# Graph attention on one core: run penalties built with fewer vector operations, one message tile moved from ScalarE to VectorE, and the third group of q rows moved ahead of the message sums on TensorE

## The chip, the cores and the metric

The kernel runs on one core of one Trainium2 chip. The metric is the device time in microseconds of one execution of the whole program. The engines are named as the profile names them: PE is TensorE (PEld its weight loads), DVE is VectorE, ACT is ScalarE, POOL is GpSimd, SP is SyncE.

## What is computed

A graph has 3125 nodes with 512 features and 50,000 edges (src, dst). Two layers follow each other; each normalises its input, applies relu and adds its result to the input. The change lies in the first layer, the attention, cut here to what matters:

```
q = (h @ Wq + bq).reshape(N, DH, NH)          # N=3125, 8 heads of 64
k = (h @ Wk + bk).reshape(N, DH, NH);  v = k
scores = einsum('edh,edh->eh', q[rows], k[cols])
m = segment_max(scores, rows)
ex = exp(scores - m[rows])
attn = ex / segment_sum(ex, rows)[rows]
out = segment_sum(attn[:, None, :] * v[cols], rows)
return out @ Wo + bo
```

The second layer sums the node rows over the other end of the edges, divides by the degree and applies two weight matrices.

## The kernel before, in words

**Stages.** The program first makes q (as three bf16 parts that add up to the f32 value) and k for all nodes, while DVE sorts the edges by node (roughly the first 385 us). Then comes the attention stage, up to about 1240 us, then the output weights, then the second layer. The change touches only the attention stage.

**Chunks.** The sorted edges are cut into windows of 125 destination nodes, and each window into chunks of CAP = 2176 edges: 128 partitions times CT = 17 tiles, with an edge's run of equal nodes lying along a partition and crossing into the next. There are 25 rounds of the function `attend` here, one for each chunk, on each engine. Round g works on two chunks at once: the scores of chunk g, and the messages (k row times weight) and their sums of chunk g-1. The order is written out by hand in each engine's block, and semaphores tie the engines together.

**One round on DVE** (`attend`, L1322 to L1381): `decode` of the next chunk's edge words (L1226 to L1235); `merge` of the former window's sums (L1304 to L1312); `messages` for the first MT = 3 tiles (L1294, two operations, one for each half of the heads); then nine groups of q rows. A group is two tiles (the last one tile). For each, L1339 multiplies the q rows in PSUM with the gathered k rows, and L1348 sums the products of the group before over the 64 features. Once the product of a group is seen to be complete, `wide_free` (L1347) lets PE overwrite its buffer. Then two scans along the partition (L1355, L1356) find the maximum of each run, with penalties of -1e30 where a run ends; `flags` (L1245 to L1263) makes the penalties for the next chunk in ten operations; two short scans (L1363, L1364) carry the maxima from partition to partition; and L1372 to L1376 add the carried maxima with their penalties, take the largest of three values and subtract it from the scores. That releases ACT (`res_ready`).

**One round on PE** (L819 to L855): two transposes for the penalties (L823), then for each of the nine groups the q rows, picked with a one-hot matrix of the edges (L834: 3 parts x 2 tiles = 6 matmuls), followed by SEG[n] tiles of message sums (L806: a tile is two matmuls, recorded as four since f32 takes two passes). The q rows alternate between two PSUM buffers, wide0 and wide1, so a group waits until DVE has finished with the group two before it (L831). After the fifth index (n == 5) come two small products for the fading factors (L816, L817). After the last group PE has two transposes (L846, L847), two more tiles, two transposes back (L851, L852) and the last four tiles.

**ACT** makes the messages of the tiles from MT to 16 with eight operations a tile (L621), and scales the window's sums (L630, L640). **POOL** gathers the k rows of the next chunk, one tile an instruction (L497), in the four parts of PARTS, and builds the one-hot tiles of the next sum (L521). A part of the row buffer is gathered only when the messages that read it are made: part 0 is released by DVE (L1343), the others by ACT (L658, L662, L667).

```
Q_GROUPS = [(t, min(2, CT - t)) for t in range(0, CT, 2)]
MT = 3
SEG = [0, 2, 1, 1, 1, 1, 1, 1, 3]
PARTS = [(0, 3), (3, 4), (7, 5), (12, CT - 12)]
```

## Time and profile before

| | us |
|---|---|
| median of 3 runs | 1978.0 (1966.38 to 1984.02) |
| the profiled execution, its time | 1975.45 |
| the profiled execution, its span | 1973.6 |
| busy in the span: PE / DVE / ACT / POOL | 1652.9 / 1367.9 / 990.9 / 1143.6 |
| mean granted TensorE clock | 0.943 of full speed |

The span runs from the first to the last instruction of the profiled execution; its own time is 1.85 us longer, for what lies around it. Times of rows are microseconds from the start of the span, a duration given as a mean is in ns. In a row of the timeline, neighbouring instructions of one kind are merged: the start, the length from the first start to the last end, and the count. An end of a matmul is modelled, and instructions of one engine overlap by a little, so a step is best read from start to start.

### The profile page before, as it was taken

Reading aid. Unit: us, or ns where it says so; the run is one execution under the profiler, and the core shown is the slowest. Engines: PE = TensorE matmul, PEld = TensorE weight load, DVE = VectorE, ACT = ScalarE, POOL = GpSimd, SP = SyncE. Lnnn points to the kernel's source line nnn. Section 1 sums busy time; section 2 is a strip of 40 time slices with the busy share of each in tenths; the row PEclk is TensorE's granted clock in tenths of the full one; section 3 lists DMA queues with packets and bytes.
Section 4 is the critical chain, followed back from the end, with each engine's and each line's share of the span. In section 5 each row is a group of like instructions: output and inputs, shape, how many; then the busy total and the mean of one; then the engine's idle time right before and its main releaser. Section 6 shows DMA issues by size and latency. Waiting matters only on the chain.

```text
span 1973.6 us, 23860 instructions
## 1 busy us (share of the span) xinstructions
PE 1652.9 (84%) x5685; PEld 953.0 (48%) x5685; DVE 1367.9 (69%) x2637; ACT 990.9 (50%) x3754; POOL 1143.6 (58%) x1322
## 2 busy tenths in 40 slices
PE   3799942289888888898889887895999999999998
PEld 1343321166666666666666666342444444444443
DVE  8789878598988898889888985465444444444441
ACT  4453310559999999999999997241000000000000
POOL 2000000487878787878787880014777777777772
PEclk9899976599999999999999999897999999999999
DMA  8122201655565656565656562935777777776773
GB/s 183 52 66 78 65 26 52 195 153 160 165 183 165 184 166 187 162 183 160 182 166 183 157 177 67 230 97 157 213 221 215 215 212 217 211 207 208 213 212 97
DMA packets 130752, 318.05 MB, mean 161 GB/s; under 512 B 39460, under 2 KB 39710, under 8 KB 130596
## 3 DMA queue, kind: packets, MB, share of 16 engines
q0 software_dynamic: 70240, 229.93, 40.6%
q1 hardware_dynamic: 60356, 86.43, 15.6%
q8 instruction: 50, 0.82, 0.2%
q14 instruction: 106, 0.87, 0.1%
HBM read 280.43 MB, written 35.86 MB: 160 GB/s over the span
## 4 chain that ended last, share of the span: by engine, by line
PE 45%; DVE 23%; DMA 13%; issue 13%; ACT 2%; SPq 2%; DVEq 1%; POOL 1%; POOLq 0%; ACTq 0%
PE wide L754 15%; PE sums L806 10%; PE wide L834 8%; PE sums L903 8%; DMA node<-h2tab 5%; DMA out<-node 4%; DVE arena L1057 3%; DVE arena L1056 3%; DVE nodes L1348 2%; DMA h2tab<-node 2%; DVE nodes L1294 1%; DVE nodes L1339 1%; DVE node L1235 1%; PE wide L749 1%; ACT arena L575 1%
## 5 line engine op out<-in xcount | busy, mean ns | idle before, releaser
L621 ACT ACTIVATE nodes<-arena,nodes 128x64 f32<-128x64 f32 x2840 | 682.7, 332 | 1.3 <-PE sums L806 1.2
L497 POOL DMA_INDIRECT arena<-ktab,idx x425 | 425.6, 1001 | 174.1 <-issue 116.3
L497 POOL DMA_INDIRECT arena<-h2tab,idx x425 | 444.8, 1047 | 140.9 <-issue 133.0
L806 PE MATMUL sums<-nodes,oh 128*125 128x260 f32 x1768 | 459.0, 402 | 41.9 <-DVE nodes L1294 41.9
L754 PE MATMUL wide<-w_sb,node 128*125 128x512 f32 x1000 | 469.5, 614 | 12.7 <-ACT node L560 9.1
L806 PEld LDWEIGHTS sums<-nodes,oh 128*125 128x125 f32 x1768 | 336.8, 195 | 116.7 <-DVE nodes L1294 53.3
L903 PE MATMUL sums<-arena,oh 128*125 128x512 f32 x850 | 373.6, 597 | 7.6 <-DMA arena<-h2tab,idx 7.6
L701 ACT ACTIVATE node<-wide 128x500 f32<-128x500 f32 x51 | 28.9, 586 | 582.6 <-PE wide L889 582.4
L834 PE MATMUL wide<-q_win,node 125*128 125x512 bf16 x1275 | 311.1, 382 | 8.4 <-issue 8.4
L754 PEld LDWEIGHTS wide<-w_sb,node 128*125 128x125 f32 x1000 | 185.6, 194 | 227.2 <-issue 209.7
L1339 DVE TENSOR_TENSOR nodes<-wide,arena 128x1024 f32<-128x1024 f32 (+1 forms) x225 | 258.7, 1159 | 12.5 <-PE wide L834 11.8
L1348 DVE TENSOR_REDUCE nodes<-nodes 128x16 f32<-128x1024 f32 (+1 forms) x225 | 256.9, 1151 | 0.0
L903 PEld LDWEIGHTS sums<-arena,oh 128*125 128x125 f32 x850 | 157.8, 188 | 203.4 <-issue 191.9
L521 POOL TENSOR_SCALAR oh<-iota,loc 128x125 f32<-128x125 f32 x425 | 245.5, 593 | 0.8
L1449 DVE SCALAR_TENSOR_TENSOR acc<-acc,first_chunk,sums 125x512 f32<-125x512 f32 x25 | 18.7, 748 | 315.2 <-PE sums L903 315.2
L834 PEld LDWEIGHTS wide<-q_win,node 125*128 125x128 bf16 x1275 | 177.9, 141 | 98.6 <-issue 12.3
L503 POOL DMA_DIRECT2D sorted_tab<-arena x2 | 1.2, 610 | 325.5 <-DVE arena L1103 325.5
L1057 DVE TENSOR_TENSOR arena<-arena 128x256 f32<-128x256 f32 x272 | 114.0, 419 | 0.0
L1056 DVE TENSOR_TENSOR arena<-arena 128x256 f32<-128x256 f32 x272 | 113.9, 419 | 0.0
L1397 DVE TENSOR_REDUCE junk<-oh 128x125 f32<-128x2125 f32 x25 | 104.1, 4163 | 0.9
L533 POOL DMA_DIRECT2D h2tab<-node x25 | 13.4, 535 | 151.9 <-ACT node L685 140.9
L1242 DVE TENSOR_TENSOR oh<-iota,loc 128x2125 f32<-128x2125 f32 x25 | 59.3, 2373 | 4.0 <-DVE loc L1233 4.0
(199 smaller groups left out, 1157.6 us busy)
## 6 DMA issues: line engine op xcount, KB each, us to landing
node<-node_tab SPq DMA_DIRECT2D x27, 531.2 KB
q_win<-qtab SPq DMA_DIRECT2D x26, 375.0 KB
arena<-ktab,idx POOLq DMA_INDIRECT x425, 5.8
arena<-h2tab,idx POOLq DMA_INDIRECT x425, 4.5
node<-h2tab SPq DMA_DIRECT2D x26, 250.0 KB
attn_tab<-win_out SPq DMA_DIRECT2D x25, 250.0 KB
h2tab<-node POOLq DMA_DIRECT2D x25, 250.0 KB, 2.9
out<-node SPq DMA_DIRECT2D x25, 250.0 KB
```

What stands on the lines that cost most here:

```text
L497: gp.indirect_dma_start(rows[:, b, t, :], None, tab, bass.IndirectOffsetOnAxis(ap=idx[:, b, t:t + 1], axis=0)).then_inc(s["rows_in"][b][PA ...
L521: last = gp.tensor_scalar(oh[:, b, t, :], iota[:, 0:WIN], loc[:, b, t + 1:t + 2], None, ALU.is_equal)
L621: last = act.activation(msgs[:, t, h // HH, h % HH * DH:(h % HH + 1) * DH], rows[:, 1 - b, t, h * DH:(h + 1) * DH], ACT.Copy, scale=den_in ...
L754: last = pe.matmul(out, ncol[:, b, c, :], w_sb[:, w, c, :], start=start and c == 0, stop=stop and c == KC - 1)
L806: last = pe.matmul(halves[:, u, :], oh[:, 1 - b, t, :], rhs[side][:, t, u, :], start=t == 0, stop=t == CT - 1)
L834: last = pe.matmul(wide[n % 2][:, (t - t0) * D:(t - t0 + 1) * D], ohT[:, b, :].rearrange("p (e t) -> p t e", t=CT)[:, t, :], q_win[:, b, p ...
L903: last = pe.matmul(aggp, oh[:, b, t, :], rows[:, b, t, :], start=t == 0, stop=t == CT - 1)
L1056: self.made(dve.tensor_tensor(new[:, :, 0, :], old[:, :, 0, :], old[:, :, 1, :], ALU.min))
L1057: self.made(dve.tensor_tensor(new[:, :, 1, :], old[:, :, 0, :], old[:, :, 1, :], ALU.max))
L1339: made.append(st.mark(dve.tensor_tensor(prod[:, n % 3, 0:k * D], wide[n % 2][:, 0:k * D], rows[:, b, t0:t0 + k, :].rearrange("p t d -> p ( ...
L1348: summed.append(st.mark(dve.tensor_reduce(sc[:, :, t0:t0 + k].rearrange("p h t -> p t h"), prod[:, (n - 1) % 3, 0:k * D].rearrange("p (t h ...
L1397: dve.tensor_reduce(oh_sum[:, b, :], oh[:, b, :, :].rearrange("p t n -> p n t"), AX.X, ALU.add).then_inc(ag["kept"], 1)
```

## The change

1. `flags` makes the penalties in five operations instead of ten. One vector `links` of 8 x 17 + 1 values per chunk, read from its first element by the forward scan and from its second by the backward scan, takes the place of two arrays of 8 x 17. The two comparisons with the end tiles become one operation, as do the two side penalties, and PE's transposes read a side penalty directly with a broadcast instead of a copy of it (`whole` is gone).
2. The two maxima `top` = max(carried0, carried1) and max(top, over) become one `tensor_reduce` over a view `three` that has the three arrays side by side in memory, 136 elements (544 bytes) apart.
3. MT goes from 3 to 4: DVE makes four message tiles, ACT thirteen. PARTS follows.
4. SEG goes from [0, 2, 1, 1, ...] to [0, 0, 2, 2, 1, ...]: PE makes the third group of q rows before any message sum, and two tiles of sums follow both the third and the fourth group. The total before the transposes stays 11 tiles.

```diff
@@ -96,15 +96,15 @@
         junk = sb("junk", [128, 2, HALF])
         scratch = junk[:, :, :].rearrange("p a c -> p (a c)")
         SEGS = CT * H
-        pen = scratch[:, 0:4 * SEGS].rearrange("p (b k h t) -> p b k h t", b=2, k=2, h=H)
-        seg_max, over, top = (scratch[:, k * SEGS:(k + 1) * SEGS].rearrange("p (h t) -> p h t", h=H) for k in (4, 5, 6))
+        links = scratch[:, 0:2 * (SEGS + 1)].rearrange("p (b s) -> p b s", b=2)
+        seg_max, top, over = (scratch[:, k * SEGS:(k + 1) * SEGS].rearrange("p (h t) -> p h t", h=H) for k in (4, 5, 6))
+        three = scratch[:, 6 * SEGS:9 * SEGS].rearrange("p (k s) -> p s k", k=3)
         carried = scratch[:, 7 * SEGS:9 * SEGS].rearrange("p (k h t) -> p k h t", k=2, h=H)
         AT = 9 * SEGS
         sides_pen = scratch[:, AT:AT + 4 * CT].rearrange("p (b k t) -> p b k t", b=2, k=2)
         same = scratch[:, AT + 4 * CT:AT + 4 * CT + CT + 1]
         same_end = scratch[:, AT + 5 * CT + 1:AT + 7 * CT + 1].rearrange("p (k t) -> p k t", k=2)
-        whole = scratch[:, AT + 7 * CT + 1:AT + 7 * CT + 1 + 4 * H].rearrange("p (b k h) -> p b k h", b=2, k=2)
-        ROWS_AT = AT + 7 * CT + 1 + 4 * H
+        ROWS_AT = AT + 7 * CT + 1
         whole_T = scratch[0:H, ROWS_AT:ROWS_AT + 256].rearrange("p (k n) -> p k n", k=2)
         from_left = scratch[0:H, ROWS_AT + 256:ROWS_AT + 256 + 2 * 129].rearrange("p (b n) -> p b n", b=2)
         from_right = scratch[0:H, ROWS_AT + 514:ROWS_AT + 514 + 129]
@@ -216,7 +216,7 @@
         QK_TURNS = [NW - 3, NW - 2]
         KEY_TURNS = [(238, 1), (251, 0), (271, 0), (286, 0)]
 
-        PARTS = [(0, 3), (3, 4), (7, 5), (12, CT - 12)]
+        PARTS = [(0, 4), (4, 3), (7, 5), (12, CT - 12)]
         PART = [max(n for n, (t0, k) in enumerate(PARTS) if t0 <= t) for t in range(CT)]
 
         def chunk_sems(p):
@@ -240,9 +240,10 @@
         fade_ready, faded_ready, others_ready, alpha_turned, alpha_ready = (sem(n) for n in ("fade_ready", "faded_ready", "others_ready", "alpha_turned", "alpha_ready"))
 
         Q_GROUPS = [(t, min(2, CT - t)) for t in range(0, CT, 2)]
-        MT = 3
+        MT = 4
+        WHOLE = (CT - 1, 0)
         TT = 12
-        SEG = [0, 2, 1, 1, 1, 1, 1, 1, 3]
+        SEG = [0, 0, 2, 2, 1, 1, 1, 1, 3]
         MID_SEG = 2
         EARLY = sum(SEG)
         assert len(SEG) == len(Q_GROUPS) and MT <= EARLY
@@ -820,7 +821,7 @@
                 pe.wait_ge(whole_ready, g + 1)
                 pe.wait_ge(alpha_ready, g + 1)
                 for k in range(2):
-                    last = pe.transpose(whole_turn[:, k, :], whole[:, b, k, :], ident[:, :])
+                    last = pe.transpose(whole_turn[:, k, :], sides_pen[:, b, k, WHOLE[k]:WHOLE[k] + 1].to_broadcast([128, H]), ident[:, :])
                 last.then_inc(whole_turned, 1)
 
                 todo = iter(range(CT))
@@ -1244,27 +1245,22 @@
 
             def flags(g, b):
 
-                st = Steps(flag_step, g, 10)
+                st = Steps(flag_step, g, 5)
                 here = loc[:, b, 1:CT + 1]
                 st.mark(dve.tensor_tensor(same, loc[:, b, 1:CT + 2], loc[:, b, 0:CT + 1], ALU.is_equal))
-                for k, t in enumerate((0, CT - 1)):
-                    st.mark(dve.tensor_scalar(same_end[:, k, :], here, here[:, t:t + 1], 1.0, ALU.is_equal, ALU.subtract))
+                st.mark(dve.tensor_tensor(same_end, here.unsqueeze(1).to_broadcast([128, 2, CT]), here[:, ::CT - 1].unsqueeze(2).to_broadcast([128, 2, CT]), ALU.is_equal))
                 st.seen(1)
-                st.then(dve.tensor_scalar(same, same, 1.0, BIG, ALU.subtract, ALU.mult))
-                for k, link in enumerate((same[:, 0:1], same[:, CT:CT + 1])):
-                    st.mark(dve.scalar_tensor_tensor(sides_pen[:, b, k, :], same_end[:, k, :], BIG, link.to_broadcast([128, CT]), ALU.mult, ALU.add))
+                st.then(dve.tensor_scalar(same, same, BIG, 2 * BIG, ALU.mult, ALU.subtract))
+                st.mark(dve.scalar_tensor_tensor(sides_pen[:, b, :, :], same_end, BIG, same[:, ::CT].unsqueeze(2).to_broadcast([128, 2, CT]), ALU.mult, ALU.add))
                 inside = same[:, 1:CT].unsqueeze(1).to_broadcast([128, H, CT - 1])
-                st.mark(dve.tensor_copy(pen[:, b, 0, :, 1:CT], inside))
-                st.mark(dve.tensor_copy(pen[:, b, 1, :, 0:CT - 1], inside))
-                st.seen(6)
-                st.mark(dve.tensor_copy(whole[:, b, 0, :], sides_pen[:, b, 0, CT - 1:CT].to_broadcast([128, H])))
-                st.then(dve.tensor_copy(whole[:, b, 1, :], sides_pen[:, b, 1, 0:1].to_broadcast([128, H])))
+                st.mark(dve.tensor_scalar(links[:, b, 0:SEGS].rearrange("p (h t) -> p h t", h=H)[:, :, 1:CT], inside, BIG, None, ALU.add))
+                st.seen(5)
                 st.end()
                 dve.sem_inc(whole_ready, 1)
 
             dve.wait_ge(consts, 3)
             firsts = [(res[:, :, :], 0.0), (acc[:, :], 0.0), (rden[:, :], 0.0), (fade[:, :], 0.0), (others[:, :, :], 0.0),
-                      (scratch[:, 0:4 * SEGS], -BIG), (from_left[:, :, :], -BIG), (from_right, -BIG)]
+                      (links[:, :, :], -BIG), (from_left[:, :, :], -BIG), (from_right, -BIG)]
             for b in range(2):
                 dve.wait_ge(store1[b], STORE1 * ((NW + 1 - b) // 2))
             for v, value in firsts:
@@ -1320,7 +1316,7 @@
                     merge(g, 1)
 
             def attend(g, b, i):
-                st = Steps(at["step"], g, 2 * len(Q_GROUPS) + 10)
+                st = Steps(at["step"], g, 2 * len(Q_GROUPS) + 9)
                 decode(at, g + 1, 1 - b, i + b, 5, 4)
                 merge_former(g, b, i)
                 dve.wait_ge(msgs_free, g + 1)
@@ -1352,8 +1348,8 @@
                 def line(v):
                     return v.rearrange("p h t -> p (h t)")
 
-                st.then(dve.tensor_tensor_scan(line(seg_max), line(pen[:, b, 0, :, :]), line(sc), -BIG, ALU.add, ALU.max))
-                st.then(dve.tensor_tensor_scan(line(over)[:, ::-1], line(pen[:, b, 1, :, :])[:, ::-1], line(seg_max)[:, ::-1], -BIG, ALU.add, ALU.max))
+                st.then(dve.tensor_tensor_scan(line(seg_max), links[:, b, 0:SEGS], line(sc), -BIG, ALU.add, ALU.max))
+                st.then(dve.tensor_tensor_scan(line(over)[:, ::-1], links[:, b, 1:SEGS + 1][:, ::-1], line(seg_max)[:, ::-1], -BIG, ALU.add, ALU.max))
                 dve.sem_inc(seg_ready, 1)
 
                 flags(g + 1, 1 - b)
@@ -1371,8 +1367,7 @@
                 dve.wait_ge(carry_turned, g + 1)
                 st.then(dve.tensor_tensor(carried, carry.unsqueeze(3).to_broadcast([128, 2, H, CT]),
                                           sides_pen[:, b, :, :].unsqueeze(2).to_broadcast([128, 2, H, CT]), ALU.add))
-                st.then(dve.tensor_tensor(top, carried[:, 0, :, :], carried[:, 1, :, :], ALU.max))
-                st.then(dve.tensor_tensor(top, top, over, ALU.max))
+                st.then(dve.tensor_reduce(line(top), three, AX.X, ALU.max))
                 st.then(dve.tensor_tensor(res[:, :, :], sc[:, :, :], top, ALU.subtract))
                 dve.sem_inc(res_ready, 1)
                 dve.wait_ge(faded_ready, g + 1)
```

PE, from the transposes at the head of a round (L823 before, L824 after) to the sixth group of q rows. L834 and L835 are the q rows, L806 and L807 the message sums; wide0 and wide1 are the two PSUM buffers. Before:

```order
L823 MATMUL wide2<-ident,junk 8x128 x2
L834 MATMUL wide0<-q_win,node 128x512 x6
L834 MATMUL wide1<-q_win,node 128x512 x6
L806 MATMUL sums<-nodes,oh 125x260 x4
L834 MATMUL wide0<-q_win,node 128x512 x6
L806 MATMUL sums<-nodes,oh 125x260 x2
L834 MATMUL wide1<-q_win,node 128x512 x6
L806 MATMUL sums<-nodes,oh 125x260 x2
L834 MATMUL wide0<-q_win,node 128x512 x6
L806 MATMUL sums<-nodes,oh 125x260 x2
L834 MATMUL wide1<-q_win,node 128x512 x6
```

After:

```order
L824 MATMUL wide2<-ident,junk 8x128 x2
L835 MATMUL wide0<-q_win,node 128x512 x6
L835 MATMUL wide1<-q_win,node 128x512 x6
L835 MATMUL wide0<-q_win,node 128x512 x6
L807 MATMUL sums<-nodes,oh 125x260 x4
L835 MATMUL wide1<-q_win,node 128x512 x6
L807 MATMUL sums<-nodes,oh 125x260 x4
L835 MATMUL wide0<-q_win,node 128x512 x6
L807 MATMUL sums<-nodes,oh 125x260 x2
L835 MATMUL wide1<-q_win,node 128x512 x6
```

The third group (the second wide0) now stands ahead of the first two tiles of sums (x4 is two tiles). The sixth group has five tiles of sums ahead of it in both; the two small products and one more tile follow it, and then the seventh group, unchanged.

DVE, from the second scan of the scores to the copy ahead of the carrying scans, before:

```order
L1356 SCALAR_TENSOR_TENSOR junk<-junk 128x136
L1249 TENSOR_TENSOR junk<-loc 128x18
L1251 TENSOR_SCALAR junk<-loc 128x17 x2
L1253 TENSOR_SCALAR junk<-junk 128x18
L1255 SCALAR_TENSOR_TENSOR junk<-junk 128x17 x2
L1257 COPY junk<-junk 128x8x16
L1258 COPY junk<-junk 128x8x16
L1260 COPY junk<-junk 128x8
L1261 COPY junk<-junk 128x8
L1360 COPY junk<-junk 8x1
```

After:

```order
L1352 SCALAR_TENSOR_TENSOR junk<-junk 128x136
L1250 TENSOR_TENSOR junk<-loc 128x18
L1251 TENSOR_TENSOR junk<-loc 128x34
L1253 TENSOR_SCALAR junk<-junk 128x18
L1254 SCALAR_TENSOR_TENSOR junk<-junk 128x34
L1256 TENSOR_SCALAR junk<-junk 128x8x16
L1356 COPY junk<-junk 8x1
```

Ten instructions between the scan and the copy (x2 counts as two) have become five.

DVE, from `others` to `fade` at the end of a round, before and after:

```order
L1369 SCALAR_TENSOR_TENSOR others<-oh,first_chunk 1x125
L1372 TENSOR_TENSOR junk<-wide,junk 128x272
L1374 TENSOR_TENSOR junk<-junk 128x136
L1375 TENSOR_TENSOR junk<-junk 128x136
L1376 TENSOR_TENSOR nodes<-nodes,junk 128x136
L1379 TENSOR_TENSOR fade<-junk 1x8
```

```order
L1365 SCALAR_TENSOR_TENSOR others<-oh,first_chunk 1x125
L1368 TENSOR_TENSOR junk<-wide,junk 128x272
L1370 TENSOR_REDUCE junk<-junk 128x136
L1371 TENSOR_TENSOR nodes<-nodes,junk 128x136
L1374 TENSOR_TENSOR fade<-junk 1x8
```

L1374 and L1375 before are L1370 after, a reduce that reads 3 x 136 values and writes 136.

## Rows read from the trace of the kernel before

**Rows 1.** Busy us of each engine in one round of the attention stage

```profile
core 0: us, PE busy (x) PEld busy (x) DVE busy (x) ACT busy (x) POOL busy (x), PEclk, DMA share, GB/s
...
711.72:744.16 32.44, 28.05 (x131) 20.42 (x130) 28.89 (x52) 31.58 (x133) 26.79 (x35) 1.00 0.62 175
```

**Rows 2.** Waits, 412 to 1172 us: engine, line, releaser, total, times, longest

```profile
PE wide L846 <- DVEq L1357: 52.2, 24, 2.3
ACT nodes L646 <- DVEq L1377: 39.4, 23, 13.8
...
POOL arena L497 <- DVEq L1343: 31.6, 22, 3.6
...
DVE nodes L1339 <- PE wide L834: 8.7, 23, 0.5
```

**Rows 3.** Timeline of DVE, round from 711.72 us: start, length, row

```profile
715.20 1.83 DVE L1294 TENSOR_TENSOR nodes<-arena,nodes 128x768 f32<-128x768 f32 x2 [0.32 <-DVE rden L1312]
716.94 2.35 DVE L1339 TENSOR_TENSOR nodes<-wide,arena 128x1024 f32<-128x1024 f32 x2
...
730.07 1.22 DVE L1339 TENSOR_TENSOR nodes<-wide,arena 128x1024 f32<-128x1024 f32 x1 [0.18 <-PE wide L834]
...
732.34 1.21 DVE L1339 TENSOR_TENSOR nodes<-wide,arena 128x1024 f32<-128x1024 f32 x1
```

**Rows 4.** Timeline of PE, same round

```profile
712.96 2.76 PE L834 MATMUL wide<-q_win,node 125*128 125x512 bf16 x12
717.08 2.02 PE L806 MATMUL sums<-nodes,oh 128*125 128x260 f32 x8 [1.36 <-DVE nodes L1294]
718.93 1.46 PE L834 MATMUL wide<-q_win,node 125*128 125x512 bf16 x6
...
728.43 1.46 PE L834 MATMUL wide<-q_win,node 125*128 125x512 bf16 x6
```

**Rows 5.** Event that frees a q buffer, L1347 (not a busy time)

```profile
L1347 DVEq EVENT_SEMAPHORE  x15: 21/21/21, 718.3 to 762.6; - x15
```

**Rows 6.** Timeline of DVE at the end of the attention stage

```profile
1207.79 6.90 DVE L1294 TENSOR_TENSOR nodes<-arena,nodes 128x1024 f32<-128x1024 f32 x6 [0.32 <-DVE rden L1312]
```

**Rows 7.** Timeline of DVE, flags and the end of the same round

```profile
738.41 0.18 DVE L1249 TENSOR_TENSOR junk<-loc 128x18 f32<-128x18 f32 x1 [0.24 <-DVE junk L1356]
...
738.78 0.17 DVE L1253 TENSOR_SCALAR junk<-junk 128x18 f32<-128x18 f32 x1
739.10 0.26 DVE L1255 SCALAR_TENSOR_TENSOR junk<-junk 128x17 f32<-128x17 f32 x2
739.28 0.22 DVE L1257 COPY junk<-junk 128x128 f32<-128x128 f32 x1
...
740.10 0.14 DVE L1360 COPY junk<-junk 8x1 f32<-8x1 f32 x1 [0.25 <-DVE junk L1261]
...
742.28 0.30 DVE L1374 TENSOR_TENSOR junk<-junk 128x136 f32<-128x136 f32 x1
...
743.23 0.30 DVE L1376 TENSOR_TENSOR nodes<-nodes,junk 128x136 f32<-128x136 f32 x1
```

**Rows 8.** Two reduces of DVE by line, shortest, median and longest in ns

```profile
L1397 DVE TENSOR_REDUCE junk<-oh x25: 4125/4166/4189, 1353.3 to 1917.9; 128x125 f32<-128x2125 f32 x25
...
L1348 DVE TENSOR_REDUCE nodes<-nodes x225: 673/1210/1217, 390.8 to 1197.2; 128x16 f32<-128x1024 f32 x100, 128x8 f32<-128x512 f32 x13
```

**Rows 9.** Timeline of PE, waits followed by slow or by full-speed matmuls

```profile
738.60 1.92 PE L806 MATMUL sums<-nodes,oh 128*125 128x260 f32 x8
...
935.56 0.28 PE L846 MATMUL wide<-ident,junk 128*8 128x128 f32 x1 [2.17 <-DVEq L1357]
...
935.78 3.47 PE L806 MATMUL sums<-nodes,oh 128*125 128x260 f32 x8
...
388.68 3.83 PE L806 MATMUL sums<-nodes,oh 128*125 128x260 f32 x8 [8.44 <-DVE nodes L1294]
...
1210.20 17.96 PE L806 MATMUL sums<-nodes,oh 128*125 128x260 f32 x68 [3.52 <-DVE nodes L1294]
```

## The prediction

> **What bounds the kernel now.** I first read the page's busy shares by slice and the starts of the rounds of `attend`: only the attention stage is touched, and its round, the stretch from 711.72 to 744.16 us, is 32.44 us. The busy times of this round come next [rows 1]: ACT 31.58, DVE 28.89, PE 28.05, POOL 26.79 plus its gather issues. ACT looks like the bound, but the list of waits says otherwise [rows 2]: ACT waits in every round for DVE's subtraction (L1377; 39.4 us over 23 rounds), POOL waits in every round for DVE's release of part 0 (L1343; 31.6 us), and PE waits for DVE's scans (L1357; 52.2 us over 24 rounds). DVE waits for another engine in one place only that counts: 23 times, 8.7 us in all, for q rows from PE (L1339 after L834). Its other idle time is behind its own instructions. So the round is DVE's chain of instructions, with PE's q rows as a second chain that it meets on the way.
>
> Where the two meet is seen in the two timelines of one round. DVE starts the two message products at 715.20, the first q product at 716.94 and the seventh at 730.07 [rows 3]: 13.13 us. Product and reduce take 2.27 us start to start when nothing is late (730.07 to 732.34 [rows 3]). From the first product to the third DVE has two products and one reduce, three steps of half of that, 3.4 us, and from there to the seventh four pairs, 9.1 us: 12.5 us in all. So DVE is about 0.6 us late by the seventh product, and it is PE that makes it late: the seventh group of q rows starts at 728.43 and lasts 1.46 us [rows 4], to 729.89, 0.18 us before the product. PE in turn works without a break from 717.08, where it had waited 1.36 us for the messages, and the two tiles of sums that it then makes take 1.85 us, up to the third group of q rows at 718.93 [rows 4].
>
> **The change part by part.**
>
> *The fourth message tile on DVE.* Two operations of 128x768 elements take 1.74 us start to start (715.20 to 716.94 [rows 3]). At 128x1024 six of them take 6.90 us [rows 6], 1.15 us each, so two take 2.30. DVE's first q product moves back by 0.55 us, from 716.94 to 717.49. ACT loses eight operations, 1/14 of its messages; since it waits for DVE already [rows 2], that buys nothing by itself. POOL's wait for part 0 is there today; the release comes 0.55 us later in the round, and a longer round gives POOL that time back: nothing. The k rows of a part are gathered in the round before, so the fourth tile of part 0 is not waited for.
>
> *The third group of q rows first.* It goes into the buffer of the first group, so it cannot start before DVE's first product is complete. The event that says so is at 718.3 [rows 5], 1.36 us after the product's start at 716.94. After the change it comes at 717.49 + 1.36 = 718.85, and PE starts about 0.05 us later, as it did behind the messages (715.20 + 1.83 = 717.03, PE at 717.08 [rows 3, 4]). So the third group starts at 718.9: exactly when it starts today, 718.93. But today two tiles of sums are done by then; after the change PE has stood still in that time and both are still to do. Every group from the fifth on has as many tiles ahead of it as before, so each starts later by two tiles. A tile is 0.87 us (eight sums of two tiles: 1.85 us less the first one's 0.1 [rows 4]), so PE comes to the seventh group at 728.43 + 1.75 = 730.18, and DVE's seventh product at 730.18 + 1.46 + 0.18 = 731.82, against 730.07: +1.75 us. DVE alone would be there at 717.49 + 12.5 = 730.0, so PE decides. The 0.55 us of the messages lie inside the 1.75. What follows the seventh product keeps its distance from it. PE's wait before L846, 2.2 us in the mean (52.2/24 [rows 2]), is the cover for its own last sums and stays. Bounds: at least +1.2 (if one tile more than I think is hidden under the wait), at most +1.9.
>
> *Flags.* Today 1.69 us pass from L1249 (738.41) to L1360 (740.10) [rows 7]. After it: the comparison ends at 738.59 and is seen 0.14 us later, 738.73; the next step takes 0.32 (738.78 to 739.10 [rows 7]), 739.05; the side penalties need 0.12 to issue, the `links` operation lasts 0.22 as L1257 does, and 0.25 of waiting follow: 739.64. That is 0.46 us less. Bounds -0.3 and -0.6. It is on DVE's chain, so it counts in full; the transposes that the carrying scans need are done at 738.8, and PE's next wait (L851) has 0.9 us of cover.
>
> *The reduce in place of two maxima.* Today 0.95 us from L1374 to L1376 [rows 7]. The reduce reads 408 values. By L1348, which reads contiguous values at 1.04 ns each, (1210 - 676 for 512 more), it lasts 0.57 us and with 0.15 until the next step 0.72: a gain of 0.23. By L1397, which also reduces over a long stride (500 bytes), it is 4166/2125 = 1.96 ns each [rows 8], 0.80 us and with 0.15 us 0.95: nothing gained. The form is that of L1397 (here 544 bytes), so I take 0. The Trainium skill, SBUF — State Buffer, in "Door 1: The DMA port swizzle", says that accesses that leave a 16-byte line each time pay a penalty, which speaks for the slow price and against this edit; L1397's 1.96 ns agree with it.
>
> *Sum of this.* 1.75 - 0.46 + 0 = +1.3 us a round. The first round starts with slow matmuls and its own order of waits; I count it as nothing. 24 rounds x 1.3 = +31 us.
>
> *TensorE's clock.* PE's wait ahead of the third group grows from 1.36 us to 718.9 - 715.72 (the end of the first twelve, 712.96 + 2.76 [rows 4]) = 3.2 us. The rows show what waits do: behind the 2.17 us before L846 the eight sums sometimes take 3.47 us instead of 1.92 (935.78 and 738.60 [rows 9]), that is the lower level, 1.2 GHz, for most of them; I count 10 of the 25 such waits of the stage with over 2.5 us behind them. Behind the waits of 3.52 and 8.44 us it was slow both times (68 sums in 17.96 us, 8 in 3.83 us [rows 9]); behind 1.36 us never (2.02 us for 8 [rows 4]). A wait of 3.2 us lies between: from 10 of 25 to all of them, and I take 18. The price is 0.7 to 1.8 us (sums of 2.6 to 3.8 us against 2.0), 1.3 in the middle, and this time it falls on the third group and the sums behind it, PE's unbroken run up to the seventh group, so it reaches DVE in full. 18 x 1.3 = +23 us. The Trainium skill, TensorE: Matmul & The Clock Gate, in "HAM oscillation — how this bites in real kernels", warns of just this, bursts behind waits that each begin at the lower clock; the 3.47 us of the trace agree.
>
> Together 31 + 23 = +54 us. Against the profiled execution's own time, 1975.45, this gives 2029.5; the median of the runs is 2.5 us above that execution, so 2032.
>
> **Rivals.**
>
> *The clock holds.* As forecast, but the 3.2 us wait costs no more than its length. For it: over half of the 2.2 us waits had no effect. Against: 3.52 us did. 1978 + 31 = 2009 us.
>
> *Faster: PE is not what makes DVE late.* The mechanism is the meeting at the third and seventh groups. If PE could keep ahead with the third group made first, DVE would lose the 0.6 us of lateness that it has today, and the round would change by +0.55 (messages) - 0.6 (lateness) - 0.46 (flags) - 0.23 (reduce at the contiguous price) = -0.75 us, 24 times: 1978 - 18 = 1960 us. It decides if the seventh group is ready by 730.0, that is if PE's run from the third group on takes 9.5 us instead of 11.3. For it: DVE's only lateness is against PE today, and the third product stops being at risk. Against: PE's rows show no gap in that run that could close.
>
> *Nothing measurable.* The messages of the tiles behind MT, made earlier by ACT, could not help PE; but PE might start the third group earlier than the event suggests, and the reduce be cheap: +1.2 - 0.6 - 0.23 = +0.4 us a round without a clock effect, 1978 + 9 = 1987 us.
>
> *The change doesn't reach the order.* The listing of PE's instructions shows the third group moved, so this is left at nothing.
>
> **How the numbers follow.** Slower with the clock effect 0.48, slower with the clock held 0.26, nothing measurable 0.13, faster 0.13. The predicted time is that of the first, 2032. The range: below, it reaches past the clock held with the cheap reduce (2009 - 6) to the third case, 1985; above, all 25 waits slow at 1.5 us and the larger bounds, 31 + 37 + 5 = +73, 2051. It leaves out the faster case and some of the third. A measurement of this kernel can tell about 1% from no change, 20 us: faster than 1958 gets 0.1 (most of the faster case and a little for what I don't see), within 1% 0.2 (the rest of that case, the third case and a part of the second), slower than 1998 0.7.
>
> **What would show it.** In the new trace the round grows from 32.5 to 33.8 us where the clock is full and by more where it falls; PE's wait ahead of its third group is about 3.2 us and ends with DVE's event behind the first product; DVE waits for q rows at the fourth or fifth and at the seventh group, 1.8 us a round together where it was 0.6; flags takes 1.2 us; the reduce lasts 0.8 us (0.57 if the stride costs nothing); ACT's wait ahead of L646 grows to over 4 us. It would be wrong if PE's third group started within 1 us of the first product's start, or if DVE's waits for q rows were not longer than before.

## The result and the profile after

| | before | after |
|---|---|---|
| median of 4 runs, us | 1978.42 (1966.38 to 1984.02) | 2032.72 (2028.53 to 2046.07) |
| profiled execution, us | 1975.45 | 2028.53 |
| granted clock, mean of the span | 0.943 | 0.93 |

The ratio is 1.0283 (95% interval 1.0249 to 1.0316): the changed kernel is 54 us slower. Ratios, here and below, compare executions in the faster state of the chip; one execution of flags and reduce alone (e10, below), 2194.37 us at a granted clock of 0.778, is left out of its ratio by that. The loss lies in the attention stage; the last stretch is 3 us shorter. Stretches of the two kernels, columns as in [rows 1], after and then before, the middle one being that stage:

```profile
0.00:385.00 385.00, 234.48 (x598) 102.28 (x598) 315.78 (x818) 137.83 (x346) 31.06 (x36) 0.84 0.31 86
385.00:1291.50 906.50, 766.59 (x3291) 554.99 (x3291) 733.17 (x1161) 733.72 (x3060) 647.87 (x837) 0.93 0.53 155
1291.50:2026.60 735.10, 675.89 (x1796) 309.92 (x1796) 322.54 (x503) 71.30 (x151) 458.81 (x450) 0.98 0.69 196
```

```profile
385.00:1235.50 850.50, 738.27 (x3292) 539.71 (x3293) 730.12 (x1316) 780.68 (x3255) 654.33 (x837) 0.97 0.57 166
```

The stage has grown from 850.5 to 906.5 us, and TensorE's mean granted clock in it has gone from 0.97 to 0.93. The busy times of the page, after:

```profile
PE 1677.0 (83%) x5685; PEld 967.2 (48%) x5685; DVE 1371.5 (68%) x2482; ACT 942.8 (47%) x3554; POOL 1137.7 (56%) x1322
...
PEclk9899975699999999999999999898899999999999
```

DVE is as busy as before (1371.5 against 1367.9 us), ACT has 48 us less to do, PE 24 us more with the same instructions. Nobody has more work; the waits have grown. The list of waits over the same 23 or 24 rounds, columns as in [rows 2]:

```profile
ACT nodes L647 <- DVEq L1372: 131.0, 23, 13.3
...
POOL arena L498 <- DVEq L1339: 89.2, 22, 5.2
...
PE wide L835 <- DVEq L1343: 63.9, 23, 3.4
...
DVE nodes L1335 <- PE wide L835: 59.2, 77, 2.4
PE wide L847 <- DVEq L1353: 52.1, 24, 2.2
...
DVE junk L1368 <- PE wide L853: 8.0, 14, 0.9
```

Against [rows 2]: DVE's waits for q rows (L1339, now L1335) have gone from 8.7 to 59.2 us, and PE has a new wait of 63.9 us (L835 behind L1343), the one ahead of the third group; ACT's wait has grown from 39.4 to 131.0 us, which shows that its relief bought nothing. One round in which the clock held ahead of the third group, DVE first, then PE, columns as in [rows 3, 4, 7]:

```profile
1056.49 2.36 DVE L1290 TENSOR_TENSOR nodes<-arena,nodes 128x1024 f32<-128x1024 f32 x2 [0.31 <-DVE rden L1308]
1058.77 2.35 DVE L1335 TENSOR_TENSOR nodes<-wide,arena 128x1024 f32<-128x1024 f32 x2
...
1064.94 1.22 DVE L1335 TENSOR_TENSOR nodes<-wide,arena 128x1024 f32<-128x1024 f32 x1 [0.44 <-PE wide L835]
...
1067.99 1.22 DVE L1335 TENSOR_TENSOR nodes<-wide,arena 128x1024 f32<-128x1024 f32 x1 [0.70 <-PE wide L835]
...
1073.06 1.22 DVE L1335 TENSOR_TENSOR nodes<-wide,arena 128x1024 f32<-128x1024 f32 x1 [0.46 <-PE wide L835]
...
1081.46 0.18 DVE L1250 TENSOR_TENSOR junk<-loc 128x18 f32<-128x18 f32 x1 [0.24 <-DVE junk L1352]
...
1081.79 0.18 DVE L1253 TENSOR_SCALAR junk<-junk 128x18 f32<-128x18 f32 x1
...
1082.68 0.14 DVE L1356 COPY junk<-junk 8x1 f32<-8x1 f32 x1 [0.24 <-DVE junk L1256]
...
1084.84 0.44 DVE L1368 TENSOR_TENSOR junk<-wide,junk 128x272 f32<-128x272 f32 x1 [0.64 <-PE wide L853]
1085.42 0.62 DVE L1370 TENSOR_REDUCE junk<-junk 128x136 f32<-128x408 f32 x1
1086.19 0.30 DVE L1371 TENSOR_TENSOR nodes<-nodes,junk 128x136 f32<-128x136 f32 x1
```

```profile
1054.92 2.75 PE L835 MATMUL wide<-q_win,node 125*128 125x512 bf16 x12
1060.20 1.51 PE L835 MATMUL wide<-q_win,node 125*128 125x512 bf16 x6 [2.52 <-DVEq L1343]
1061.55 1.92 PE L807 MATMUL sums<-nodes,oh 128*125 128x260 f32 x8
...
1066.35 1.46 PE L835 MATMUL wide<-q_win,node 125*128 125x512 bf16 x6
...
1071.42 1.46 PE L835 MATMUL wide<-q_win,node 125*128 125x512 bf16 x6
...
1081.43 0.28 PE L847 MATMUL wide<-ident,junk 128*8 128x128 f32 x1 [2.21 <-DVEq L1353]
...
1081.65 2.84 PE L807 MATMUL sums<-nodes,oh 128*125 128x260 f32 x8
```

The third group starts at 1060.20, 1.43 us after DVE's first product (1058.77), as the event allows; the seventh product comes at 1073.06, 14.29 us after the first, where it was 13.13 [rows 3]. DVE waits three times on the way, 0.44, 0.70 and 0.46 us. Flags takes 1.22 us (1081.46 to 1082.68), where it took 1.69 [rows 7], and the reduce with its step 0.77 us where two maxima took 0.95. The round, from one start of `attend` to the next, is 34.20 us. In other rounds the clock falls behind PE's wait ahead of the third group:

```profile
600.88 2.55 PE L835 MATMUL wide<-q_win,node 125*128 125x512 bf16 x6 [3.03 <-DVEq L1343]
```

Its six matmuls take 2.55 us instead of 1.51, the sums behind them are slow too, and one of DVE's waits for q rows grows from 0.44 to 1.49 us:

```profile
607.31 1.22 DVE L1335 TENSOR_TENSOR nodes<-wide,arena 128x1024 f32<-128x1024 f32 x1 [1.49 <-PE wide L835]
```

From the first to the seventh product this round takes 15.97 us. That distance is 14.29 or 14.30 us in 11 of the 24 rounds after the first and 15.9 to 17.1 us in the other 13, 23.2 us more in sum.

The sum over 23 rounds closes. The mean round (first and last start 419.67 and 1226.69 us after, 417.81 and 1172.58 before) has gone from 32.82 to 35.09 us, +2.27. The parts are +0.54 (fourth tile: 1056.49 to 1058.77 is 2.28 us, against 1.74 in [rows 3]), -0.47, -0.18, (59.2 - 8.7)/23 = +2.20 for the waits for q rows and (8.0 - 3.5)/23 = +0.20 for the waits of L1368: +2.29.

### The profile page after: what moved, and what is told of

Same layout as the page of the kernel before. It is cut to its first block, busy times and chain, and to the rows that moved or that the text cites. A ratio compares the mean times of both kernels' runs of the same rounds, so it can differ in the third digit from the quotient of the medians.

```text
span 2026.6 us, 23454 instructions
## 1 busy us (share of the span) xinstructions
PE 1677.0 (83%) x5685; PEld 967.2 (48%) x5685; DVE 1371.5 (68%) x2482; ACT 942.8 (47%) x3554; POOL 1137.7 (56%) x1322
## 4 chain that ended last, share of the span: by engine, by line
PE 46%; DVE 21%; issue 14%; DMA 12%; POOL 3%; ACT 2%; SPq 2%; DVEq 1%; POOLq 0%; ACTq 0%
PE wide L755 14%; PE sums L807 13%; PE wide L835 9%; PE sums L904 7%; DMA node<-h2tab 4%; DMA out<-node 4%; POOL arena L498 3%; DVE arena L1058 2%; DVE arena L1057 2%; DVE nodes L1344 2%; DMA h2tab<-node 2%; DVE nodes L1290 2%; DVE nodes L1335 1%; PE wide L750 1%; ACT arena L576 1%
## 5 line engine op out<-in xcount | busy, mean ns | idle before, releaser
L622 ACT ACTIVATE nodes<-arena,nodes 128x64 f32<-128x64 f32 x2640 | 635.0, 332 | 2.1 <-PE sums L807 2.0
L498 POOL DMA_INDIRECT arena<-ktab,idx x425 | 417.2, 982 | 235.2 <-issue 121.3
L755 PE MATMUL wide<-w_sb,node 128*125 128x512 f32 x1000 | 464.8, 608 | 14.6 <-ACT node L561 10.4
L807 PE MATMUL sums<-nodes,oh 128*125 128x260 f32 x1768 | 472.0, 413 | 3.5 <-DVE nodes L1290 3.5
L835 PE MATMUL wide<-q_win,node 125*128 125x512 bf16 x1275 | 322.8, 392 | 85.2 <-DVEq L1343 77.2
L807 PEld LDWEIGHTS sums<-nodes,oh 128*125 128x125 f32 x1768 | 351.8, 203 | 74.8 <-DVE nodes L1290 3.6
L1335 DVE TENSOR_TENSOR nodes<-wide,arena 128x1024 f32<-128x1024 f32 (+1 forms) x225 | 258.6, 1158 | 65.2 <-PE wide L835 65.2
L835 PEld LDWEIGHTS wide<-q_win,node 125*128 125x128 bf16 x1275 | 177.3, 142 | 189.9 <-DVEq L1343 88.8
L1392 DVE TENSOR_REDUCE junk<-oh 128x125 f32<-128x2125 f32 x25 | 104.1, 4164 | 0.9
L534 POOL DMA_DIRECT2D h2tab<-node x25 | 13.4, 535 | 153.1 <-ACT node L686 146.1
L647 ACT ACTIVATE nodes<-nodes 128x136 f32<-128x136 f32 x26 | 11.2, 432 | 180.4 <-DVEq L1372 140.2
```

What stands on the lines that cost most here:

```text
L498: gp.indirect_dma_start(rows[:, b, t, :], None, tab, bass.IndirectOffsetOnAxis(ap=idx[:, b, t:t + 1], axis=0)).then_inc(s["rows_in"][b][PA ...
L622: last = act.activation(msgs[:, t, h // HH, h % HH * DH:(h % HH + 1) * DH], rows[:, 1 - b, t, h * DH:(h + 1) * DH], ACT.Copy, scale=den_in ...
L755: last = pe.matmul(out, ncol[:, b, c, :], w_sb[:, w, c, :], start=start and c == 0, stop=stop and c == KC - 1)
L807: last = pe.matmul(halves[:, u, :], oh[:, 1 - b, t, :], rhs[side][:, t, u, :], start=t == 0, stop=t == CT - 1)
L835: last = pe.matmul(wide[n % 2][:, (t - t0) * D:(t - t0 + 1) * D], ohT[:, b, :].rearrange("p (e t) -> p t e", t=CT)[:, t, :], q_win[:, b, p ...
L1335: made.append(st.mark(dve.tensor_tensor(prod[:, n % 3, 0:k * D], wide[n % 2][:, 0:k * D], rows[:, b, t0:t0 + k, :].rearrange("p t d -> p ( ...
```

## The experiments

The kernel before was run beside each experiment, on the same chip. In two of the five sessions it took 1977 us, as above. In the other three, on chips 1 and 11, it took 2195 to 2257 us, at a granted clock of 0.89 to 0.91 instead of 0.94. Those are told separately below, since there something else sets the round. The first fences below are from the sessions at 1977 us.

### What the clock costs: PE kept busy in its new wait

```diff
                 for n, (t0, k) in enumerate(Q_GROUPS):
+                    if n == 2:
+                        pe.wait_ge(at["acc_free"], g + 1)
+                        for _ in range(20):
+                            pe.transpose(tiny[:, 0:128], ident[:, :], ident[:, :])
                     pe.wait_ge(wide_free, g * len(Q_GROUPS) + n + 1)
```

> The changed kernel, with PE kept busy by 20 dummy transposes (about 0.12 us each, 2.3 us) into an unused corner of PSUM in its wait ahead of the third group; nothing else moves. Theory (that wait lets TensorE's clock fall to 1.2 GHz in half of the rounds): the slow matmuls behind it vanish, rounds go from 35.2 in the mean to about 34.2 us, and the time falls by about 20 to 25 us against the changed kernel (ratio to before 1.016 to 1.020 instead of 1.028). Rival (the clock falls for another reason, or costs nothing here): no change against the changed kernel, ratio 1.028.

Measured: 2007.84 us (before 1977.52), ratio 1.0165 (1.014 to 1.0189): 25 us less than the changed kernel by the medians, 23 by the ratios. The third group behind the shorter wait runs at full speed in all 24 rounds (after the first), as here:

```profile
528.51 1.51 PE L839 MATMUL wide<-q_win,node 125*128 125x512 bf16 x6 [0.85 <-DVEq L1347]
```

So TensorE's clock in this one wait is worth 23 to 25 us of the 54. The mean round is 34.1 us, as expected, but it is made of two kinds. Clean rounds are 33.58 us, which is 32.44 + 1.24 + 0.54 - 0.65, the other parts of the sum. Nine of the 24 are 34.7 to 35.0 us, and their rows show a place that I had not priced:

```profile
514.94 0.28 PE L851 MATMUL wide<-ident,junk 128*8 128x128 f32 x1 [2.20 <-DVEq L1357]
...
515.16 3.59 PE L807 MATMUL sums<-nodes,oh 128*125 128x260 f32 x8
518.68 0.22 PE L856 MATMUL wide<-ident,junk 8*128 8x8 f32 x1
```

```profile
519.00 0.44 DVE L1372 TENSOR_TENSOR junk<-wide,junk 128x272 f32<-128x272 f32 x1 [1.29 <-PE wide L857]
```

The clock also falls in the 2.2 us wait ahead of the two transposes (L847 after, L851 in this kernel), the eight sums take 3.59 us, and DVE then waits 1.29 us at the carry (L1372, where it takes the carried maxima; L1368 after) for the transposes that stand behind them. Over 23 rounds that wait is 10.1 us, in 9 of them.

### Order undone, the rest kept

```diff
-        SEG = [0, 0, 2, 2, 1, 1, 1, 1, 3]
+        SEG = [0, 2, 1, 1, 1, 1, 1, 1, 3]
```

> The changed kernel with PE's old order [0, 2, 1, 1, 1, 1, 1, 1, 3], again on a chip where the kernel before takes about 1978 us. Theory: +0.55 for the fourth tile, -0.65 for flags and reduce: 1976, up to 1985 if PE's wait of 1.9 us for the messages lets the clock fall; ratio 0.998 to 1.004. Rival (the parts add up in another way and the order is not the cause): ratio over 1.01.

Measured: 1985.81 us (before 1977.23), ratio 1.0042 (1.002 to 1.0064). Undoing one list gives back 47 of the 54 us: the order is the cause. The distance from the first to the seventh product is back at 13.05 us in each undisturbed round:

```profile
455.52 2.35 DVE L1335 TENSOR_TENSOR nodes<-wide,arena 128x1024 f32<-128x1024 f32 x2
...
468.57 1.22 DVE L1335 TENSOR_TENSOR nodes<-wide,arena 128x1024 f32<-128x1024 f32 x1 [0.38 <-PE wide L835]
```

The time is just above the 1976 to 1985 us that were expected. PE's wait for the messages is 1.24 to 1.8 us in most rounds and 2.0 to 2.3 in four; behind just these four the sums are slow:

```profile
555.24 2.91 PE L807 MATMUL sums<-nodes,oh 128*125 128x260 f32 x8 [2.31 <-DVE nodes L1290]
```

That is the smaller part of what the theory lacks. The profiled execution, 1994.86 us, is one of the slower of the ten, and its list of waits, columns as in [rows 2], has

```profile
DVE nodes L1335 <- PE wide L835: 15.6, 27, 1.7
DVE junk L1368 <- PE wide L853: 13.5, 13, 1.3
```

against 8.7 and 3.5 us before: 7 us more for q rows, 10 us more at the carry. The sums behind the wait ahead of L847 are slow in 15 of the 25 rounds here and in 10 before.

### Flags and reduce alone

From the changed kernel:

```diff
-        PARTS = [(0, 4), (4, 3), (7, 5), (12, CT - 12)]
+        PARTS = [(0, 3), (3, 4), (7, 5), (12, CT - 12)]
-        MT = 4
+        MT = 3
-        SEG = [0, 0, 2, 2, 1, 1, 1, 1, 3]
+        SEG = [0, 2, 1, 1, 1, 1, 1, 1, 3]
```

> Only the five-operation flags and the single reduce, tile split and order as before. Theory: 0.47 + 0.18 us less on DVE's chain in each of 24 rounds, 16 us, of which POOL's own cycle may keep 1: about 1963, ratio 0.992. Rival (DVE's chain gains nothing because ACT, with 31.6 us of work in a round of 32.4, or POOL becomes the bound at once): ratio 0.998 or more.

Measured: 1966.44 us (before 1977.23), ratio 0.9949 (0.9925 to 0.9973): 10 us faster than the kernel before, and the fastest of the versions that ran at 1977 us. The clean rounds are 31.79 us, 32.44 less the 0.65 expected. Where the other 6 us went is, as far as the waits show it, again the wait ahead of L847. From its list of waits, columns as in [rows 2]:

```profile
PE wide L847 <- DVEq L1353: 50.0, 23, 2.2
...
ACT nodes L647 <- DVEq L1372: 14.3, 22, 1.4
...
DVE junk L1368 <- PE wide L853: 8.8, 9, 1.3
```

The same wait in the kernel before, over 412 to 1172 us:

```profile
DVE junk L1372 <- PE wide L852: 3.5, 9, 0.8
```

DVE waits at the carry for 8.8 us in 9 rounds; before it was 3.5 us in 9, so 5.3 us more. The shorter flags bring DVE to the carry 0.47 us sooner, but the slow sums of a fallen clock don't move with it: in those rounds (33.0 us) the gain is lost again. ACT still waits in 22 of 23 rounds, so it is not what holds the time.

Taken from these, with after at 1978 x 1.0283 = 2034: flags and reduce -10 us, the fourth tile 1986 - 1968 = +18, the order 2034 - 1986 = +48 (ratios times 1978). They are differences: the order alone and the tile alone did not run in a session at 1977 us, so the order's share is shown with the other edits in place.

### Three sessions in which the kernel before took 2195 to 2257 us

Nine kernels ran there. First the parts one by one, and the order undone. e1 is e10's kernel and e4 is e9's; e2 and e3 start from the kernel before:

```diff
-        SEG = [0, 2, 1, 1, 1, 1, 1, 1, 3]
+        SEG = [0, 0, 2, 2, 1, 1, 1, 1, 3]
```

```diff
-        PARTS = [(0, 3), (3, 4), (7, 5), (12, CT - 12)]
+        PARTS = [(0, 4), (4, 3), (7, 5), (12, CT - 12)]
-        MT = 3
+        MT = 4
```

> Only the five-operation flags and the single reduce are kept; the tile split (3 on DVE, 14 on ACT) and PE's order are those of before. Theory (the order on PE makes the loss, the other edits shorten DVE's chain by 0.47 + 0.18 = 0.65 us a round): 24 x 0.65 = 16 us faster than before, about 1962; POOL's own cycle of 31.85 us (its wait of 0.89 instead of the usual 0.30 gives back 0.59) may keep 1 us of that. Rival (the new penalties cost something, such as the longer strides): 1978 or more.

> The kernel before with PE's new order of q rows and sums alone. Theory: from the first to the seventh q product the round takes 14.3 us instead of 13.1, +1.16 x 24 = +28 us, and the wait ahead of the third group, about 2.6 us here, makes the clock fall in a part of the rounds and adds 5 to 25 us more: 2011 to 2031, about 2020. Rival (the fourth tile on DVE is what costs): within 5 us of 1978.

> The kernel before with the fourth tile on DVE and the row parts to match, alone. Theory: DVE's and PE's chains both start 0.55 us later, +0.55 x 24 = +13 us: 1991, and PE's wait for the messages grows from 1.4 to 1.9 us, which may cost up to 6 us by the clock. Rival (the tile is the main cause of the loss): 2015 or more. Rival (ACT was the bound and gains 1.9 us): 1970 or less.

> The changed kernel with PE's old order. Theory: +0.55 - 0.65 = -0.1 us a round, 1976, or up to 1985 if PE's wait of 1.9 us for the messages lets the clock fall. The undoing of this one list then gives back 48 to 57 us of 54. Rival (the parts add up in another way): over 2000.

Measured, against 2256.84 us: 0.9969 (0.9917 to 1.0021), 0.9893 (0.9817 to 0.9969), 0.9925 (0.9891 to 0.9959) and 0.9863 (0.9789 to 0.9937). The order's 42 us and the tile's 13 are not to be seen, the order alone is even a little faster, and e1's interval is too wide to tell its 16 us (0.993) from nothing. Here other waits set the round. Two lines of the waits with the order undone, and one round's start:

```profile
POOL arena L498 <- DVEq L1339: 134.0, 20, 6.9
...
DVE den L1302 <- remote: 36.7, 21, 2.5
```

```profile
724.86 0.16 DVE L1302 TENSOR_TENSOR den<-den,sums 125x8 f32<-125x8 f32 x1 [1.46 <-remote]
...
739.86 1.22 DVE L1335 TENSOR_TENSOR nodes<-wide,arena 128x1024 f32<-128x1024 f32 x1 [1.28 <-PE wide L835]
```

```profile
736.76 1.46 PE L835 MATMUL wide<-q_win,node 125*128 125x512 bf16 x6
```

DVE waits 36.7 us for something that the profile puts down to no engine of the core, and starts its fifth product (739.86) 1.6 us after PE has finished the rows for it (736.76 + 1.46). The last stage, where none of these edits reaches, is slower as well: ACT's wait there for PE, in this run first and then in e9's, which is the same kernel:

```profile
ACT node L702 <- PE wide L890: 715.2, 45, 46.0
```

```profile
ACT node L702 <- PE wide L890: 590.8, 41, 27.2
```

I could not settle what is slower in these sessions. It is not fixed by the chip either: chip 11 gave 2194.87 us for the kernel before in one of them and 2254.0 us in the next. Their comparisons say nothing for or against the theory of the others.

A second group of four ran against 2194.87 us, and one more against 2254.0.

```diff
-        SEG = [0, 0, 2, 2, 1, 1, 1, 1, 3]
+        SEG = [0, 0, 2, 1, 1, 1, 1, 1, 4]
```

> The changed kernel with one of the two tiles behind the fourth group moved to the end of the run, SEG = [0, 0, 2, 1, 1, 1, 1, 1, 4]; the third group stays ahead and PE's wait in front of it stays. Theory (the loss is the number of tiles PE must still do before the seventh group once the third has started): 0.87 us less in each of 24 rounds, 21 us off the changed kernel's 2033, about 2012, ratio 1.017, perhaps 5 us better still because PE's wait ahead of L847 shrinks by the same 0.87 us and the clock falls less there. Rival (the loss comes from the wait ahead of the third group alone): ratio 1.028.

Measured 2212.0 us, ratio 1.0068 (1.0016 to 1.0119); the time is no test here. All 25 rounds take 16.1 to 16.5 us from first to seventh product, where the theory has 14.29 - 0.87 = 13.4. PE's wait ahead of the third group is 5 us here instead of 2.5 to 3.35, and the matmuls behind it are slow in each round:

```profile
PE wide L835 <- DVEq L1343: 104.3, 21, 5.2
```

What one tile is worth is thus not measured.

> Flags and reduce only, order and tile split of before, and 14 dummy transposes (1.6 us) on PE in its 2.15 us wait ahead of L847. Theory (flags and reduce give their full 0.65 us, but half of the rounds lose up to 1.2 us, because the clock falls in that wait and the slow sums delay the transposes that DVE waits for at L1368): all rounds 31.8 us, 16 to 22 us faster than before, ratio 0.989 to 0.992. Rival (ACT or POOL takes back the gain): no better than without the filler, 0.995.

> Flags and reduce, three tiles on DVE, SEG = [0, 1, 1, 1, 1, 1, 1, 1, 4] so that the third group has one tile ahead of it instead of two and DVE is never late for q rows, and 10 dummy transposes ahead of L847. Theory: DVE's chain 32.44 - 0.65 - 0.6 = 31.2 us, ACT's 31.6 us of work then decides: 0.2 us a round better than e8, ratio 0.987 to 0.990. Rival (the third group is bound by DVE's release as before and nothing is gained): as e8.

Measured 2274.8 us, 1.0365 (1.0277 to 1.0453), and 2280.92 us, 1.0372 (1.0296 to 1.0448): both miss what was expected, by far. Both have three tiles on DVE, and the edit that they share beyond e1's kernel is this, ahead of the two transposes:

```diff
+                for _ in range(14):
+                    pe.transpose(wide[2][:, 384:512], ident[:, :], ident[:, :])
                 pe.wait_ge(seg_ready, g + 1)
```

e11 has 10 dummies instead of 14 and SEG = [0, 1, 1, 1, 1, 1, 1, 1, 4]. Most of their rounds are 41.0 us. DVE waits 4.25 us at the carry, though PE's transposes start at 730.42 and 730.48 and last 0.2 us each (e8):

```profile
734.89 0.44 DVE L1370 TENSOR_TENSOR junk<-wide,junk 128x272 f32<-128x272 f32 x1 [4.25 <-remote]
```

```profile
723.85 1.69 PE L847 MATMUL wide<-ident 128*128 128x128 f32 x14
...
730.42 0.20 PE L854 MATMUL wide<-ident,junk 8*128 8x8 f32 x1 [2.12 <-issue]
...
730.61 5.46 PE L807 MATMUL sums<-nodes,oh 128*125 128x260 f32 x16
```

The sums behind them take 5.46 us where a round at full clock has 3.77. In e8 the wait at the carry is 104.1 us in 20 rounds; in e1, the same kernel without the dummies but in another session, it was 31.4 us in 18. What the added instructions meet there no run tells. So whether the filler would give flags and reduce their full 16 us in a session at 1977 us stays open, and so does e11's order.

The last two move tiles of sums to the end, e12 from the changed kernel with e5's filler, e13 from e10:

```diff
-        SEG = [0, 0, 2, 2, 1, 1, 1, 1, 3]
+        SEG = [0, 0, 1, 1, 1, 1, 1, 1, 5]
```

> The changed kernel (four tiles on DVE, third group first) with two tiles moved behind, SEG = [0, 0, 1, 1, 1, 1, 1, 1, 5], and the filler of 20 transposes in the wait ahead of the third group. Theory: the 1.8 us that DVE is late by the seventh product vanish, rounds go from 33.6 to 31.8 us, about 1963, ratio 0.993: the third group first is harmless if as many tiles go behind. Rival (the third group first costs by itself, or the five tiles at the end delay the transposes): ratio over 1.00.

Measured 2199.56 us (before 2194.87), 0.9976 (0.9927 to 1.0025). That contains the theory's 0.993 and reaches the rival's 1.00: it decides nothing.

```diff
-        SEG = [0, 2, 1, 1, 1, 1, 1, 1, 3]
+        SEG = [0, 1, 1, 1, 1, 1, 1, 1, 4]
```

> Flags and reduce only, three tiles on DVE, and one tile of sums moved from ahead of the third group to the end, SEG = [0, 1, 1, 1, 1, 1, 1, 1, 4]; no filler. Theory (DVE's lateness at the seventh product is the number of tiles PE does before it): the 0.6 us of lateness goes, PE's wait ahead of L847 shrinks from 2.2 to about 1.6 us so that the clock falls there less often, and ACT's 31.6 us of work becomes the bound: rounds 31.6 us, 18 to 22 us faster than before, ratio 0.989 to 0.991, against 0.9949 for flags and reduce alone. Rival (the tiles ahead of the third group fill a wait that is there anyway, so moving one gains nothing): 0.995.

Measured 2239.08 us (before 2254.0), 0.9858 (0.9803 to 0.9913). The ratio is even below that of its theory, but in such a session, where e1 and e2 ran against theirs, I don't count it as shown. It is the version to try next where the kernel before takes 1977 us.

## Why the prediction was right

The time was 2032.72 us where 2032 was predicted, and the way it comes about is the one forecast. Point by point:

- **DVE's chain sets the round and PE's q rows meet it at the seventh product.** Right: where the clock holds, 14.29 us from first to seventh product with the new order, 13.05 with the old one (e9), and 47 of 54 us come back with the old list. The +1.75 us, fourth tile included, were +1.24 + 0.54 = 1.78.
- **The third group starts when DVE's event allows, 1.4 us after the first product.** Right: 1.43 us.
- **Flags.** -0.46 forecast, -0.47 measured.
- **The reduce.** The step that priced it by L1397, the reduce over 500-byte steps, was wrong: it lasts 0.62 us for 408 values, 1.5 ns each with its fixed part, and with the step behind it 0.77 us; the gain is 0.18 us a round and not 0. That is the size that L1348's contiguous values give (0.57). The rule of the Trainium skill, SBUF — State Buffer, in "Door 1: The DMA port swizzle", that values over 16 bytes apart are dearer, does not show in this instruction.
- **TensorE's clock behind the new wait.** The mechanism is right and is shown by e5, worth 23 to 25 us (23 forecast). That the size fits is luck, since its two factors were each off: 13 of 24 rounds fell instead of 18, and a fallen one cost 1.8 us (23.2/13) instead of 1.3. The wait was 2.5 to 3.35 us and not 3.2 in all rounds. In the 2.5 us rounds PE comes late to it, because the wait ahead of L847 had already let the clock fall: the sums behind that wait were slow in front of each of the eight waits under 2.6 us.
- **"PE's next wait (L851) has 0.9 us of cover".** This was the weak step. It held at the full clock only. With slow sums behind the wait ahead of L847 and flags 0.47 us shorter, DVE waits at the carry: 8.0 us in 14 rounds after the change, 8.8 us in e10, 10.1 us in e5, 13.5 us in e9, up to 1.3 us in a round, where it was 3.5 us before. It took 5 to 6 of the 16 us that flags and reduce should give by themselves. In the sum it was hidden by the reduce's gain that I had left out.
- **The first round** was counted as nothing and cost 2.0 us (34.63 against 32.65): its first matmuls are slow for longer than those of the kernel before.
- **ACT and POOL** buy nothing: as forecast, both wait longer. ACT's wait ahead of L647 is 4.48 us in the round shown.

The total was closer than its terms, and that too is luck. The reduce gave 4 us that were not counted, the carry and the first round took 5 and 2 that were not, and the last stretch is 3 us shorter (735.1 against 738.1 us), for which I have no cause.

## What to carry to other kernels

When two engines hand work to each other in a fixed order, count what the late engine must still do before the next meeting point from the moment its input allows it to start. Work that filled a wait before and is now queued behind it costs its whole length, even if the total is unchanged. On TensorE a longer wait can cost twice, since the matmuls behind it may run at the lower clock, as 13 of 24 rounds did here; and whoever shortens a chain on another engine should ask whether the cover that it leaves still holds at that lower clock.

## What the runs showed of the hardware that I had not expected

- A reduce on DVE over three values 544 bytes apart costs 0.62 us for 408 values in all 25 instances, while L1397, 17 values 500 bytes apart per output, costs 1.96 ns a value [rows 8]. The stride alone does not explain L1397.
- On TensorE, waits of 2.1 to 2.3 us ahead of L847 (L846 before) were followed by slow sums in 10 of 25 cases before, 17 of 25 after, 9 in e5, 15 in e9 and 11 in e10. Waits for the messages of 0.7 to 1.8 us (before, e9) were followed by slow sums in none, those of 2.04 to 2.31 us in e9 in all four. Ahead of the third group of the changed kernel, waits of 2.52 to 2.65 us were followed by full speed, those of 2.66 to 2.70 us by either, those of 2.74 to 3.35 us by the lower clock. So the length of the wait alone does not decide it.
- Sessions differ. The kernel before took 1977 or 1978 us in three of them, the first measurement among them, and 2195 to 2257 us in three others, at a granted clock of 0.89 to 0.91 instead of 0.94, and there the effect of the order was gone. A comparison holds for the session that it was made in.
